# A decoder layer on one core: the order of work ahead of the attention loop

## The chip, the cores and the metric

The kernel runs on one core of a Trainium2 chip. The metric is device time in microseconds (us), the median of several executions; lower is better. TensorE does matrix products, VectorE, ScalarE and GpSimd (called POOL in the profile) the rest, SyncE issues most transfers. Each engine runs its own list of instructions in order and waits on semaphores for the others.

## The reference

Sixteen sequences of 128 tokens with 128 features go through three sub-layers, each followed by a layer norm:

- a linear attention with a feed-forward part (`_L0_attn_ref`): `x1 = layernorm(x + attn(x))`;
- a cross attention on `ctx_1024` with 16 heads of 8 features. Queries and keys are normalised per head, the queries rotated by position and scaled, then softmax and values;
- a mixture of 8 experts, of which each token takes two.

```python
q = _layernorm(q, qn_w, qn_b)
k = _layernorm(k, kn_w, kn_b)
q = _apply_rope(q) * scale
attn = jnp.einsum('bhqd,bhkd->bhqk', q, k)
attn = jax.nn.softmax(attn, axis=-1)
o = jnp.einsum('bhqk,bhkd->bhqd', attn, v)
```

## The kernel before

Everything is float32 outside the score products. The 16 sequences are four groups (`G = 4`) of four; a group's tile is 128 partitions x 512 columns. Cross attention's queries pass these steps per group `g`, all on tensors of 128 x 512:

- VectorE `first_sum(g)` adds the first sub-layer's output and takes the means and variances of x1; ScalarE `inv_std(2, g)` makes 1/std by Ln and Exp (L854, L856); VectorE `normalise_x1(g)` writes N in four operations (L1089);
- TensorE `x1_T(g)` transposes N (L410), ScalarE `copy_x1T(g)` copies it to LNT (L896), TensorE `queries(g)` projects (L565);
- ScalarE `square(1, g, ...)` writes V (the projection with its bias, L869) and its square into QP (L870); TensorE `variances(1, g)` averages the square per head (L482); ScalarE `head_inv_std(1, g)` makes 1/std by Ln and Exp on KP (L874, L876); VectorE `head_norm(1, g)` multiplies V by KP (L1109);
- POOL `query_affine(g)` applies the norm's weight and bias to V (L1433) and forms V times cos in ADD (L1435); TensorE `rotate(g)` multiplies V by the rotation matrix (L575); VectorE `add_rotation(g)` multiplies that by sin (`times_sin`, L1175) and adds it to ADD (L1183);
- the result is split into three bfloat16 parts: ScalarE `high_part` (L884) and `middle_part` (L888), POOL `low` (L1411, L1413). SyncE writes the parts to a scratch in HBM (L347) and reads them back packed as QPK (L354, `read_packed`). The keys took the same way before, into KPK.

The attention is done in 64 units, four per sequence `b`: unit `u` is a quarter of the heads of sequence `u // 4`. For each unit the scores are computed twice. First as `scores_for_max` (L650), four products per unit, two units at a time; VectorE `maxima(u)` reduces them to the row maxima M (L1204). After a sequence's four units TensorE `max_T(b)` transposes M (L667), ScalarE `negate_max(b)` writes NEGM (L977) and issues its transfer into a row of QPK (L980), which then carries the negated maximum. After that come `scores(u, m)` (L685), whose products include this row, and ScalarE takes Exp (L1019); `times_v` (L707) multiplies with the values. The maxima run `LEAD = 12` units ahead: 12 units are done ahead of the loop, and in the loop each `scores(u, u + LEAD)` computes unit `u`'s scores and unit `u + 12`'s scores for the maximum.

A rule on banks sets the turns ahead of the loop: the scores for the maxima have two PSUM banks, so `scores_for_max(u)` waits until `maxima(u - 1)` is done (s_max), the first pair also until the packed keys and queries of group 0 have landed. `max_T(b)` waits for maxima `4b + 3` and for the negation of `b - 1`.

`keep_clock(n)` issues n products of the identity with itself into a bank of its own (L416); they compute nothing that is used. The order on each engine is written out by hand: TensorE's at L748 to L772, ScalarE's behind its last table load at L983, VectorE's in the loop over LEAD at L1279.

```python
if u >= 2:
    pe.wait_ge(s_max, u - 1)
```

(from `wait_for_max(u)`, called for `u` and `u + 1` ahead of each pair.)

Of the kernel before, what the change touches and what calls it, by code (L numbers as in the profile page):

```python
# [94 lines left out]
def decoder_layer(nc, x, ctx_in, attn_w, w1, w2, col_params, row_params, xw, eW1, eb1, eW2, eb2, consts, ones_row,  # L95
# [6 lines left out]
    with ExitStack() as ctx:  # L102
# [3 lines left out]
        def sem(name):  # L106
            return ctx.enter_context(nc.semaphore(name))
# [59 lines left out]
        QBC, KBC, B2C = (cols[:, i:i + 1] for i in range(16, 19))  # L167
# [42 lines left out]
        def cs(g):  # L210
            return slice(g * W, (g + 1) * W)

        def blk(t, b):
            return t[:, b * P:(b + 1) * P]
# [7 lines left out]
        def head_bank(t, g):  # L222

            return ((1, 1, 2, 3)[g] if t else (6 if g < G - 1 else 0))

        def var_bank(t, g):

            return (0, 0, 4, 5)[g] if t else (7 if g < G - 1 else 1)

        def x1_bank(g):  # L230

            return (0, 0, 4, 5)[g]

        def rot_bank(g):

            return (1, 6, 4, 6)[g]
# [55 lines left out]
        s_qc = sem("s_qc"); s_rot = sem("s_rot"); s_t1 = sem("s_t1"); s_t2 = sem("s_t2"); s_qh = sem("s_qh")  # L292
# [111 lines left out]
        def _(pe):  # L404
            mm = nc.tensor.matmul

            def transposes(bank, src, g, done, k=GB):

                for j in range(k):
                    last = nc.tensor.transpose(ps[:, bank, j * P:(j + 1) * P], blk(src, g * GB + j), K["ident"])  # L410
                last.then_inc(done, 1)

            def keep_clock(n, bank=7):

                for _ in range(n):
                    mm(ps[:, bank, 0:P], K["ident"], K["ident"], start=True, stop=True)  # L416
# [61 lines left out]
            def variances(t, g):  # L478
                pe.wait_ge(s_sq[t], g + 1)
                if t == 0:  # L480
                    pe.wait_ge(s_vaug, g + 1)
                mm(ps[:, var_bank(t, g), :], K["mean8"], SQ[t][:, cs(g)], start=True, stop=True).then_inc(s_var[t], 1)  # L482
# [72 lines left out]
            def x1_T(g):  # L555
                pe.wait_ge(s_norm[2], g + 1)
                if g >= 2:
                    pe.wait_ge(s_g1, NF * G)
                transposes(x1_bank(g), N, g, s_nT[2])

            def queries(g):
                pe.wait_ge(s_lnT[2], g + 1)
                if g >= 2:
                    pe.wait_ge(s_g2, g + 1)
                mm(ps[:, head_bank(1, g), :], XWT[:, 0, :], LNT[:, cs(g)], start=True, stop=True).then_inc(s_qc, 1)  # L565

            def rotate(g):
                pe.wait_ge(s_aff[1], g + 1)
                if g == 1:
                    pe.wait_ge(s_g1, NF * G)  # L570
                if g == 2:
                    pe.wait_ge(s_lv[1], 3)
                if g == 3:
                    pe.wait_ge(s_t2, 2)
                mm(ps[:, rot_bank(g), :], K["rotate"], V[:, cs(g)], start=True, stop=True).then_inc(s_rot, 1)  # L575
# [58 lines left out]
            def wait_for_max(u):  # L634

                b = u // 4
                if u % (4 * GB) == 0:
                    pe.wait_ge(s_pack[0][b // GB], 32)
                    pe.wait_ge(s_pack[1][b // GB], 32)
                if u == 0:  # L640
                    pe.wait_ge(s_lv[1], 2)
                if u == 1:
                    pe.wait_ge(s_sq[1], 2)
                if u >= 2:
                    pe.wait_ge(s_max, u - 1)

            def score_for_max(u, j):
                b, par, half = max_unit(u)
                t = slice(b * P, (b + 1) * P)
                last = mm(ps[:, u % 2, j * P:(j + 1) * P], QPK[HALF * par:HALF * par + KROWS, 4 * half + j, t],  # L650
                          KPK[HALF * par:HALF * par + KROWS, 4 * half + j, t], start=True, stop=True)
                if j == 3:
                    last.then_inc(s_sm, 1)

            def scores_for_max(u):

                wait_for_max(u)
                wait_for_max(u + 1)
                for j in range(4):
                    score_for_max(u, j)  # L660
                    score_for_max(u + 1, j)

            def max_T(b):
                pe.wait_ge(s_max, 4 * (b + 1))
                if b >= 1:
                    pe.wait_ge(s_negm, b)
                nc.tensor.transpose(ps[0:H, 7, 0:P], M[:, b % RING, :], K["ident"]).then_inc(s_mT, 1)  # L667
# [79 lines left out]

            pe.wait_ge(s_g1, NF * G)  # L748
            x1_T(2)
            keep_clock(6)  # L750
            queries(2)
            scores_for_max(0)
            keep_clock(4)
            scores_for_max(2)
            keep_clock(3)
            x1_T(3)
            variances(1, 2)
            scores_for_max(4)
            keep_clock(2)
            queries(3)  # L760
            scores_for_max(6)
            keep_clock(3)
            max_T(0)
            variances(1, 3)
            scores_for_max(8)
            pe.wait_ge(s_negm, 1)
            keep_clock(3)
            max_T(1)
            scores_for_max(10)
            pe.wait_ge(s_negm, 2)  # L770
            keep_clock(4)
            rotate(2)  # L772
            for u in range(4 * B):
                b, r = divmod(u, 4)
                scores(u, u + LEAD)
# [71 lines left out]
        def _(act):  # L847
            A = nc.scalar.activation

            def inv_std(n, g, eps):  # L850

                act.wait_ge(s_mv[n], g + 1)
                b = slice(g * GB, (g + 1) * GB)
                A(lnv[:, n, b], mv[:, n, b, 1], ACT.Ln, bias=eps).then_inc(s_lnv[n], 1)  # L854
                act.wait_ge(s_lnv[n], g + 1)
                A(rstd[:, n, b], lnv[:, n, b], ACT.Exp, scale=-0.5).then_inc(s_rstd[n], 1)  # L856
# [9 lines left out]
            def square(t, g, done_mm, bias):  # L866
                act.wait_ge(done_mm, g + 1)
                if t == 1:
                    A(V[:, cs(g)], ps[:, head_bank(t, g), :], ACT.Identity, bias=bias)  # L869
                A(SQ[t][:, cs(g)], ps[:, head_bank(t, g), :], ACT.Square, bias=bias).then_inc(s_sq[t], 1)  # L870

            def head_inv_std(t, g):
                act.wait_ge(s_var[t], g + 1)
                A(RS[t][:, cs(g)], ps[:, var_bank(t, g), :], ACT.Ln, bias=1e-6).then_inc(s_lv[t], 1)  # L874
                act.wait_ge(s_lv[t], g + 1)
                A(RS[t][:, cs(g)], RS[t][:, cs(g)], ACT.Exp, scale=-0.5).then_inc(s_rs[t], 1)  # L876

            def high_part(t, g):
                act.wait_ge((s_aff[0], s_qh)[t], g + 1)
                if g >= 2:  # L880
                    act.wait_ge(s_scr[t][g % 2], 16 * len(TERMS_K) * (g // 2))
                if t == 1 and g < 2:
                    act.wait_ge(s_scr[0][g % 2], 16 * len(TERMS_K) * (G // 2))
                nc.scalar.copy(PART[:, g % 2, 0, :], (KN, ADD)[t][:, cs(g)]).then_inc(s_hi[t], 1)  # L884

            def middle_part(t, g):
                act.wait_ge(s_r1[t], g + 1)
                nc.scalar.copy(PART[:, g % 2, 1, :], (KQ, KP)[t][:, cs(g)]).then_inc(s_mid[t], 1)  # L888
# [5 lines left out]
            def copy_x1T(g):  # L894
                act.wait_ge(s_nT[2], g + 1)
                nc.scalar.copy(LNT[:, cs(g)], ps[:, x1_bank(g), :]).then_inc(s_lnT[2], 1)  # L896
# [85 lines left out]

            copy_x1T(2)  # L983
            high_part(1, 1)
            inv_std(2, 3, 1e-5)
            square(1, 2, s_qc, QBC)
            middle_part(1, 1)
            copy_x1T(3)
            head_inv_std(1, 2)
            square(1, 3, s_qc, QBC)  # L990
            negate_max(0)
            head_inv_std(1, 3)
# [77 lines left out]
        def _(dve):  # L1070
# [14 lines left out]
            def normalise(dst, src, n, g, ready, done):  # L1085
                dve.wait_ge(ready, g + 1)
                for j in range(GB):
                    b = g * GB + j
                    last = ts(dst(b), src(b), mv[:, n, b, 0:1], rstd[:, n, b:b + 1], ALU.subtract, ALU.mult)  # L1089
                last.then_inc(done, 1)  # L1090
# [79 lines left out]
            def normalise_x1(g):  # L1170
                normalise(lambda b: blk(N, b), lambda b: blk(LNT, b), 2, g, s_rstd[2], s_norm[2])
# [94 lines left out]
            def place(g):  # L1266
# [9 lines left out]
                step(nc.vector.tensor_reduce(HH, rank[:, :, :], AX.X, ALU.add))  # L1276
                nc.vector.tensor_copy(posu[:, bs], HH).then_inc(s_pos, 1)

            for u in range(LEAD):  # L1279
                maxima(u)  # L1280
                if u == 1:
                    normalise_x1(3)
                if u == 5:
                    head_norm(1, 2, QBC)
                if u == 8:
                    head_norm(1, 3, QBC)
            add_rotation(2)
            for u in range(4 * B):
# [313 lines left out]
```

## Time and profile before

| | us |
|---|---|
| median of 3 runs | 318.08 (318.07 to 318.13) |
| the profiled execution | 315.94 |
| its span, first to last instruction | 313.9 |
| TensorE busy | 259.9 |
| VectorE busy | 182.2 |
| ScalarE busy | 152.5 |
| POOL busy | 109.2 |

The median is what counts; the profiled execution is one run with the profiler on, and its span is what the views show. Busy times of the engines overlap. The chain that ended last is the work followed back from the last instruction, at each step to what released it; 63% of the span is TensorE's on it, 10% VectorE's, 9% ScalarE's and 6% transfers. In a timeline "x4" means that four like instructions were merged; a float32 product shows as two records, so an identity product counts 2. Two operations of an engine can overlap by about 0.1 us in the records. "issue" in the chain is time in which the engine waited for nothing that the profile shows; a wait for a transfer may be put down to it.

### The profile page before, as it was taken

How to read it: one execution, taken by the hardware profiler on the slowest of the kernel's cores; microseconds unless marked ns; L12 is line 12 of the kernel's file. 1: busy time of each engine (PE TensorE's matmuls, PEld its weight loads, DVE VectorE, ACT ScalarE, POOL GpSimd, SP SyncE). 2: the span in 40 equal slices, each digit the busy share in tenths (PEclk: the TensorE clock that was granted, in tenths of full speed). 3: DMA queues.
4: the chain of work that ended last, by engine and by line, in shares of the span. 5: the costliest groups of instructions: out<-in, count | busy, mean ns of one | idle time of the engine just before them, and what ended most of it. 6: DMA issues, size and time to landing. Idle time of an engine off the chain costs nothing.

```text
span 313.9 us, 7318 instructions
## 1 busy us (share of the span) xinstructions
PE 259.9 (83%) x2359; PEld 191.9 (61%) x2359; DVE 182.2 (58%) x649; ACT 152.5 (49%) x375; POOL 109.2 (35%) x164
## 2 busy tenths in 40 slices
PE   0697877968999997799988998981699999999980
PEld 0376755843453445445554555681699999999970
DVE  4732474872034466687769788568056666666660
ACT  2234216446689784367666767520044444444430
POOL 4000003720432441546400815755124444434431
PEclk9999999999999999989999999996599999999997
DMA  7910203530599775436790001151222200000000
GB/s 209 294 43 0 72 0 101 151 51 1 148 216 179 281 148 136 70 82 122 219 194 4 3 3 39 37 154 34 60 60 70 68 17 17 17 20 14 3 16 17
DMA packets 26641, 26.43 MB, mean 84 GB/s; under 512 B 2895, under 2 KB 23120, under 8 KB 26610
## 3 DMA queue, kind: packets, MB, share of 16 engines
q1 hardware_dynamic: 24996, 23.25, 31.2%
q0 software_dynamic: 1328, 2.75, 2.5%
q8 instruction: 16, 0.26, 0.4%
q14 instruction: 13, 0.11, 0.1%
q10 hardware_dynamic: 288, 0.07, 0.1%
HBM read 16.93 MB, written 9.29 MB: 84 GB/s over the span
## 4 chain that ended last, share of the span: by engine, by line
PE 63%; DVE 10%; ACT 9%; DMA 6%; issue 5%; POOL 2%; SPq 1%; ACTq 1%; POOLq 1%; DVEq 0%
PE ps L842 11%; PE ps L831 10%; PE ps L685 4%; PE ps L416 4%; PE ps L707 4%; PE ps L584 3%; DMA WA<-in_attn_w_dram 3%; DMA QPK<-NEGM 2%; PE ps L438 2%; PE ps L551 2%; PE ps L410 2%; PE ps L482 2%; DVE N L1089 2%; PE ps L575 2%; PE ps L723 2%
## 5 line engine op out<-in xcount | busy, mean ns | idle before, releaser
L1204 DVE TENSOR_REDUCE M<-ps 128x4 f32<-128x512 f32 x64 | 42.8, 685 | 14.9 <-PE ps L650 14.2
L1019 ACT ACTIVATE CTX<-ps 128x512 f32<-128x512 f32 x64 | 37.6, 602 | 23.7 <-PE ps L685 16.9
L1060 ACT ACTIVATE KPK<-ps,EB 128x128 f32<-128x128 f32 x80 | 24.6, 358 | 37.6 <-PE ps L831 33.8
L831 PE MATMUL ps<-QPK,EW 128*128 x320 | 39.6, 277 | 0.4 <-ACT QPK L1045 0.4
L842 PE MATMUL ps<-EW,KPK 128*128 128x128 f32 x320 | 39.4, 276 | 0.0
L831 PEld LDWEIGHTS ps<-QPK,EW 128*128 128x128 f32 x320 | 37.8, 194 | 0.8 <-issue 0.8
L1536 POOL DMA_INDIRECT out_dram<-ADD,tok_u x21 | 21.0, 1002 | 49.3 <-DVE ADD L1370 49.3
L842 PEld LDWEIGHTS ps<-EW,KPK 128*128 128x128 f32 x320 | 37.2, 191 | 0.0
L416 PE MATMUL ps<-C 128*128 128x128 f32 x178 | 27.8, 301 | 7.1 <-DMA sorted_scratch<-KVS,posu 7.1
L416 PEld LDWEIGHTS ps<-C 128*128 128x128 f32 x178 | 23.7, 205 | 10.5 <-issue 9.9
L685 PE MATMUL ps<-QPK,KPK 49*128 49x128 bf16 x256 | 25.4, 221 | 2.7 <-ACT CTX L1019 1.6
L650 PE MATMUL ps<-KPK,QPK 48*128 48x128 bf16 x256 | 23.1, 221 | 4.2 <-DVE M L1204 2.2
L685 PEld LDWEIGHTS ps<-QPK,KPK 49*128 49x128 bf16 x256 | 14.6, 95 | 14.7 <-issue 10.1
L1378 DVE TENSOR_SCALAR KPK<-ps,EB 128x128 f32<-128x128 f32 x80 | 22.3, 336 | 0.5 <-PE ps L831 0.5
L1516 POOL DMA_INDIRECT sorted_scratch<-KVS,posu x16 | 15.6, 976 | 19.3 <-PE ps L685 8.5
L650 PEld LDWEIGHTS ps<-KPK,QPK 48*128 48x128 bf16 x256 | 13.3, 95 | 7.7 <-DVE M L1204 4.9
L410 PE MATMUL ps<-C,N 128*128 128x128 f32 x48 | 8.5, 305 | 11.1 <-DVE N L1089 11.0
L1384 DVE SCALAR_TENSOR_TENSOR ADD<-ps,ADD 128x128 f32<-128x128 f32 x20 | 5.8, 291 | 17.5 <-PE ps L842 16.6
L551 PE MATMUL ps<-LNT,W 128*128 128x512 f32 x32 | 14.6, 595 | 0.9 <-ACT QPK L952 0.9
L410 PEld LDWEIGHTS ps<-C,N 128*128 128x128 f32 x48 | 6.0, 153 | 13.3 <-issue 8.6
L707 PE MATMUL ps<-CTX,VA 128*32 128x128 f32 x256 | 13.9, 285 | 0.0
L1166 DVE TENSOR_TENSOR LNT<-ps,X 128x512 f32<-128x512 f32 x4 | 2.8, 689 | 18.8 <-PE ps L410 18.8
(215 smaller groups left out, 492.6 us busy)
## 6 DMA issues: line engine op xcount, KB each, us to landing
k_packed_scratch<-PART SPq DMA_DIRECT2D x24, 128.0 KB, 2.4
KPK<-k_packed_scratch SPq DMA_DIRECT2D x8, 384.0 KB, 6.5
q_packed_scratch<-PART SPq DMA_DIRECT2D x24, 128.0 KB, 2.8
QPK<-q_packed_scratch SPq DMA_DIRECT2D x8, 384.0 KB, 5.7
EW<-in_eW_dram SPq DMA_DIRECT2D x1, 2048.0 KB, 12.4
KPK<-sorted_scratch SPq DMA_DIRECT2D x24, 66.0 KB, 1.9
X<-in_x_dram SPq DMA_DIRECT2D x4, 256.0 KB, 4.2
C<-in_constants_dram SPq DMA_DIRECT2D x1, 720.0 KB, 6.2
```

Source lines behind the costliest of these rows:

```text
L416: mm(ps[:, bank, 0:P], K["ident"], K["ident"], start=True, stop=True)
L551: mm(ps[:, 4 + c, :], W1[:, c * P:(c + 1) * P], LNT[:, cs(g)], start=True, stop=True).then_inc(s_f1, 1)
L650: last = mm(ps[:, u % 2, j * P:(j + 1) * P], QPK[HALF * par:HALF * par + KROWS, 4 * half + j, t], KPK[HALF * par:HALF * par + KROWS, 4 * h ...
L685: last = mm(ps[:, 2 + u % 2, j * P:(j + 1) * P], KPK[HALF * par:HALF * par + KROWS + 1, 4 * half + j, t], QPK[HALF * par:HALF * par + KROW ...
L707: last = mm(ps[TILE * j:TILE * (j + 1), 5 + b % 2, half * P:(half + 1) * P], VA[b // 8][:, c:c + TILE], EXPS[:, u % 4, j * P:(j + 1) * P], ...
L831: last = mm(ps[:, c // 2, (c % 2) * P:(c % 2 + 1) * P], EW1[:, e, (c % NF) * P:(c % NF + 1) * P], XST[:, bass.ds(t * P, P)], start=True, s ...
L842: last = mm(ps[:, 4, 0:P], HE[:, c, :], EW2[:, e, c % NF, :], start=(c == 0), stop=(c == 2 * NF - 1))
L1019: A(EXPS[:, u % 4, :], ps[:, 2 + u % 2, :], ACT.Exp).then_inc(s_exp, 1)
L1060: last = A(HE[:, c, :], ps[:, k, (c % 2) * P:(c % 2 + 1) * P], ACT.Relu, bias=EB1[:, h, c:c + 1])
L1204: nc.vector.tensor_reduce(M[:, b % RING, c:c + 4], bank_rows(u % 2), AX.X, ALU.max).then_inc(s_max, 1)
L1378: last = ts(HE[:, NF + c, :], ps[:, 2 + k, (c % 2) * P:(c % 2 + 1) * P], EB1[:, (h + 1) % NE, c:c + 1], 0.0, ALU.add, ALU.max)
L1536: pool.indirect_dma_start(out_rows, bass.IndirectOffsetOnAxis(ap=tok_u[:, 0:1], axis=0), OUTN[:, :], None, bounds_check=last_row, oob_is_e ...
```

## The change

Three lists of instructions are reordered and `keep_clock` is redistributed; nothing else changes.

```diff
--- before.py
+++ after.py
@@ -747,29 +747,29 @@
 
             pe.wait_ge(s_g1, NF * G)
             x1_T(2)
-            keep_clock(6)
+            keep_clock(3)
             queries(2)
+            keep_clock(5)
+            variances(1, 2)
+            keep_clock(2)
+            x1_T(3)
             scores_for_max(0)
-            keep_clock(4)
+            queries(3)
             scores_for_max(2)
-            keep_clock(3)
-            x1_T(3)
-            variances(1, 2)
+            keep_clock(2)
             scores_for_max(4)
-            keep_clock(2)
-            queries(3)
-            scores_for_max(6)
-            keep_clock(3)
             max_T(0)
             variances(1, 3)
-            scores_for_max(8)
+            scores_for_max(6)
             pe.wait_ge(s_negm, 1)
             keep_clock(3)
+            rotate(2)
+            scores_for_max(8)
             max_T(1)
+            pe.wait_ge(s_negm, 2)
+            keep_clock(3)
             scores_for_max(10)
-            pe.wait_ge(s_negm, 2)
-            keep_clock(4)
-            rotate(2)
+            keep_clock(2)
             for u in range(4 * B):
                 b, r = divmod(u, 4)
                 scores(u, u + LEAD)
@@ -982,11 +982,11 @@
 
             copy_x1T(2)
             high_part(1, 1)
+            square(1, 2, s_qc, QBC)
             inv_std(2, 3, 1e-5)
-            square(1, 2, s_qc, QBC)
             middle_part(1, 1)
+            head_inv_std(1, 2)
             copy_x1T(3)
-            head_inv_std(1, 2)
             square(1, 3, s_qc, QBC)
             negate_max(0)
             head_inv_std(1, 3)
@@ -1276,13 +1276,12 @@
                 step(nc.vector.tensor_reduce(HH, rank[:, :, :], AX.X, ALU.add))
                 nc.vector.tensor_copy(posu[:, bs], HH).then_inc(s_pos, 1)
 
+            normalise_x1(3)
             for u in range(LEAD):
                 maxima(u)
                 if u == 1:
-                    normalise_x1(3)
-                if u == 5:
                     head_norm(1, 2, QBC)
-                if u == 8:
+                if u == 7:
                     head_norm(1, 3, QBC)
             add_rotation(2)
             for u in range(4 * B):
```

On TensorE, behind `x1_T(2)` (its transposes are the first row): L416 is `keep_clock`, L565 `queries`, L482 `variances(1, 2)`, the second L410 `x1_T(3)`, and L650 x8 a pair of scores for the maxima. The last two rows are `queries(2)` and the first pair before, `queries(3)` and the second pair now.

```order
 L410 MATMUL ps<-C,N 128x128 x4
-L416 MATMUL ps<-C 128x128 x6
+L416 MATMUL ps<-C 128x128 x3
+L565 MATMUL ps<-LNT,XWT 128x512
+L416 MATMUL ps<-C 128x128 x5
+L482 MATMUL ps<-QP,C 128x512
+L416 MATMUL ps<-C 128x128 x2
+L410 MATMUL ps<-C,N 128x128 x4
+L650 MATMUL ps<-KPK,QPK 128x128 x8
 L565 MATMUL ps<-LNT,XWT 128x512
 L650 MATMUL ps<-KPK,QPK 128x128 x8
```

The first scores moved from behind `queries(2)` to behind `variances(1, 2)` and `x1_T(3)`; `queries(3)` moved up from between the third and the fourth pair to between the first and the second.

On TensorE just ahead of the loop, whose first `scores` is L685: L667 is `max_T(1)` and L575 `rotate(2)`. The L650 x8 in both is the sixth pair before and the fifth now; the one with a + is the sixth now.

```order
 L416 MATMUL ps<-C 128x128 x3
-L667 MATMUL ps<-C,M 16x128
+L575 MATMUL ps<-V,C 128x512
 L650 MATMUL ps<-KPK,QPK 128x128 x8
-L416 MATMUL ps<-C 128x128 x4
-L575 MATMUL ps<-V,C 128x512
+L667 MATMUL ps<-C,M 16x128
+L416 MATMUL ps<-C 128x128 x3
+L650 MATMUL ps<-KPK,QPK 128x128 x8
+L416 MATMUL ps<-C 128x128 x2
 L685 MATMUL ps<-QPK,KPK 128x128
```

`rotate(2)` moved from between the last pair and the loop to ahead of the fifth pair, and the identity products at the entry are three ahead of the sixth pair and two behind it, where four stood behind it.

On VectorE, behind the statistics of group 3 (L1082): L1204 is `maxima`, L1089 `normalise_x1(3)`, L1109 `head_norm`.

```order
 L1082 BN_AGGR mv<-st 128x2 x4
-L1204 TENSOR_REDUCE M<-ps 128x4 x2
 L1089 TENSOR_SCALAR N<-LNT,mv,rstd 128x128 x4
-L1204 TENSOR_REDUCE M<-ps 128x4 x4
+L1204 TENSOR_REDUCE M<-ps 128x4 x2
 L1109 TENSOR_TENSOR V<-V,KP 128x512
-L1204 TENSOR_REDUCE M<-ps 128x4 x3
+L1204 TENSOR_REDUCE M<-ps 128x4 x6
 L1109 TENSOR_TENSOR V<-V,KP 128x512
```

The normalisation stands ahead of all maxima; `head_norm(1, 2)` is behind the second maximum instead of the sixth, and `head_norm(1, 3)` behind the eighth instead of the ninth.

## Rows read from the trace of the kernel before

**Rows 1.** The page, part 2: TensorE's granted clock in 40 equal slices.
```profile
PEclk9999999999999999989999999996599999999997
```

**Rows 2.** The chain that ended last: start us, length us, what (xcount).
```profile
117.19 1.97 issue
...
122.28 0.44 PE ps L410 x4
...
128.91 0.64 ACT KP L876
129.57 0.69 DVE V L1109
```

**Rows 3.** Windows: stretch, us, busy PE, PEld, DVE, ACT, POOL, PEclk, DMA, GB/s.
```profile
129.00:131.00 2.00, 0.19 (x2) 0.02 (x1) 1.29 (x2) 0.69 (x2) 0.64 (x1) 1.00 0.04 6
...
132.20:135.60 3.40, 3.40 (x22) 1.70 (x21) 1.62 (x3) 0.60 (x1) 0.28 (x1) 0.50 0.00 0
```

**Rows 4.** Timeline to the second scores: start us, us, engine line op.
```profile
114.82 1.50 PE L416 MATMUL ps<-C 128*128 128x128 f32 x12
...
115.02 0.58 ACT L896 COPY LNT<-ps 128x512 f32<-128x512 f32 x1 [0.17 <-PE ps L410]
...
116.16 1.02 PE L565 MATMUL ps<-LNT,XWT 128*128 128x512 f32 x2
...
117.69 0.20 ACT L856 ACTIVATE rstd<-lnv 128x4 f32<-128x4 f32 x1
117.81 0.67 ACT L869 ACTIVATE V<-ps,cols 128x512 f32<-128x512 f32 x1
118.37 0.68 ACT L870 ACTIVATE QP<-ps,cols 128x512 f32<-128x512 f32 x1
...
119.16 0.40 PE L650 MATMUL ps<-KPK,QPK 48*128 48x128 bf16 x8 [1.97 <-issue]
...
119.58 1.29 DVE L1204 TENSOR_REDUCE M<-ps 128x4 f32<-128x512 f32 x2 [2.16 <-PE ps L650]
...
120.79 1.11 DVE L1089 TENSOR_SCALAR N<-LNT,mv,rstd 128x128 f32<-128x128 f32 x4
...
121.01 0.40 PE L650 MATMUL ps<-KPK,QPK 48*128 48x128 bf16 x8 [0.36 <-DVE M L1204]
```

**Rows 5.** Timeline: VectorE's normalisation and POOL's operations near it.
```profile
111.86 1.40 DVE L1089 TENSOR_SCALAR N<-LNT,mv,rstd 128x128 f32<-128x128 f32 x4
112.05 0.89 POOL L1433 TENSOR_SCALAR V<-V,cols 128x512 f32<-128x512 f32 x1 [2.17 <-DVE V L1109]
...
119.64 1.16 POOL L1413 TENSOR_TENSOR PART<-KP,PART 128x512 bf16<-128x512 f32 x1 [2.12 <-ACT PART L888]
```

**Rows 6.** Timeline at the loop's entry.
```profile
127.08 1.15 ACTq L980 DMA_DIRECT2D QPK<-NEGM  x1
...
131.01 0.40 PE L650 MATMUL ps<-KPK,QPK 48*128 48x128 bf16 x8 [1.82 <-DVE M L1204]
...
131.34 1.31 PE L416 MATMUL ps<-C 128*128 128x128 f32 x8
...
132.44 1.92 PE L575 MATMUL ps<-V,C 128*128 128x512 f32 x2
...
134.29 0.28 PE L685 MATMUL ps<-QPK,KPK 49*128 49x128 bf16 x1
...
134.39 0.69 DVE L1175 TENSOR_TENSOR QP<-ps,C 128x512 f32<-128x512 f32 x1 [1.68 <-PE ps L575]
...
135.80 1.28 DVE L1204 TENSOR_REDUCE M<-ps 128x4 f32<-128x512 f32 x2
```

**Rows 7.** SyncE's timeline of group 1's and 3's reads; chain at 157 us.
```profile
123.14 1.23 SPq L354 DMA_DIRECT2D QPK<-q_packed_scratch  x2
...
154.12 1.22 SPq L354 DMA_DIRECT2D QPK<-q_packed_scratch  x2
...
157.23 7.70 DMA QPK<-NEGM
```

## The prediction

> **What bounds the kernel now.** I read four views, in this order. First the page: its slices of the granted clock show TensorE at 9 in all but four of 40; the first of the four, an 8, is the eighteenth slice, 133 to 141 us, where the kernel enters its attention loop [rows 1]. Then the chain of waits around that place. It lies on TensorE, with three kinds of piece between: 1.97 us of waiting until the packed queries of group 0 had landed, then group 3's head variances (ScalarE's Ln and Exp on KP, 0.6 us each), then VectorE's product V times KP that stands between two maxima [rows 2]. The last of these counts: `head_norm(1, 3)` starts at 129.57, as soon as ScalarE has its 1/std, and the ninth `maxima` waits behind it. TensorE, whose next scores need ten maxima, is idle 1.82 us and starts at 131.01 [rows 6].
>
> Third the windows: from 129 to 131 us TensorE was busy for 0.19 us; from 132.2 to 135.6 its granted clock was 0.50, so 1.2 GHz instead of 2.4 [rows 3]. The price shows in one operation: `rotate(2)` takes 1.92 us at 132.44, where the product of the same size in `queries(2)` took 1.02 at 116.16 [rows 4, 6]. Last the timeline, for lengths and order. The first scores start at 119.16, the second pair at 121.01: one turn (scores, two maxima, a semaphore) is 1.85 us [rows 4]. Six pairs need five turns and the first maximum of the last, 5 x 1.85 + 0.42 + 0.61 + 0.14 = 10.4 us; the loop could start at 129.6. It starts at 134.29 [rows 6]. So 4.7 us are lost to waits, slow clock and work laid in the wrong place.
>
> **The change, walked through.** I move each instruction to where its inputs let it start, with lengths of the same operation.
>
> Start. `x1_T(2)` is as before, so the identity products begin at 114.82. Six took 1.34 us up to 116.16, 0.22 each [rows 4]; three are done at 115.5. `queries(2)` then waits only for ScalarE's copy, over at 115.60, and runs 115.65 to 116.67 instead of from 116.16: 0.5 earlier. ScalarE now squares group 2 first: V at 116.7, the square 0.56 behind it and 0.68 long [rows 4], done at 117.95. `inv_std(2, 3)` (two of 0.20) comes after it, at 118.3 instead of 117.89: the price of that swap is 0.4. VectorE was idle then, so `normalise_x1(3)` costs its own length, 1.11 alone [rows 4] or 1.40 beside POOL [rows 5]; POOL's second part of group 1 now falls on it, so I take the middle: done at 119.55. TensorE fills with five products and `variances(1, 2)`, over before 119.2, then two more. `x1_T(3)` starts at 119.7 and takes 0.44 [rows 2], and the first scores start at 120.15. Before it was 119.16: **1.0 us lost**. The packed queries, which set 119.16, have landed by then.
>
> Turns. `queries(3)` needs the copy of group 3, which ScalarE makes after Ln and Exp for group 2 (119.2 to 120.4): copy to 121.0, queries 121.1 to 122.05. The second scores could start at 120.15 + 1.85 = 122.0, so this costs 0.05. `head_norm(1, 2)` (0.69) lies in the gap in which VectorE waits for those scores: nothing. Third scores at 123.9, fourth at 125.75, with `max_T(0)` and `variances(1, 3)` between them while VectorE takes maxima. ScalarE issues the row of block 0 at 124.85; that instruction took 1.15 [rows 6] and Ln and Exp for group 3 stand behind it: done at 127.25. `head_norm(1, 3)` starts after the eighth maximum, 127.45, and ends at 128.15. Three products and `rotate(2)` run 126.1 to 127.8 under the maxima; fifth scores at 127.8 instead of 127.6, 0.2 lost. Sixth at 129.65. `scores(0)` needs eleven maxima: 129.65 + 0.42 + 0.61 + 0.14 is 130.85. The walk is 120.15 + 5 x 1.85 + 0.25 + 1.2. Against 134.29 that is **3.45 us earlier**, made of the idle 1.82 gone, `rotate(2)` (1.92) and four products (1.1 from 131.34) off the entry, 1.0 and 0.4 of the turns lost again.
>
> Into the loop. Before, `rotate(2)` ended just ahead of the loop, and from VectorE's `times_sin(2)` at 134.39 to its next maximum at 135.80 are 1.41 us, 1.51 behind the loop's start [rows 6]. Now `times_sin(2)` waits for the twelfth maximum, 131.35, and the thirteenth starts at 132.75, 1.9 behind the start. So **0.4 is given back**, while `rotate(3)` at full clock hides in it; ScalarE's second Exp, behind the cast of VectorE's sum (`high_part(1, 2)`), moves with VectorE. From the thirteenth maximum on both kernels run the same instructions, 3.05 us apart. SyncE's transfers of groups 2 and 3 hang on that cast and shift with it. There are 25 identity products before and 20 now; the last two lie in the 0.9 us in which TensorE waits for the eleventh maximum.
>
> Sum: +1.0 late first scores, -4.45 of waits and entry work, +0.4 into the loop: -3.05. Profiled execution: 315.94 (span 313.9) to 312.9. The runs' median, 318.08, is 2.1 above the profiled one; I subtract from the median: **315.0 us**. Ends: if group 3's statistics and the normalisation go faster than walked, and the loop gives nothing back, -4.2; if each of the eight links from `queries(2)` to the first scores costs 0.1 more, -2.2.
>
> **Rivals.**
>
> A. *The clock falls all the same.* TensorE now waits about 0.6, then 1.0 us between pairs; 1.82 idle came before the fall, but 1.97 at 117.19 came before none [rows 2, 6], so a length of idling alone does not tell. For: little work is added there. Against: no wait is above 1.0, and the fillers sit in the gaps. A stretch like the one seen (3.4 us at 0.50, all busy [rows 3]) loses half, 1.7: -1.35, 316.7 us. Chance 0.11.
>
> B. *The row of block 0 lands late.* `scores(0)` needs NEGM's row in QPK. It is issued at 124.85 instead of 127.08, now inside the reads of group 1's queries, which SyncE issued at 123.14 [rows 7]. The trace has a row that landed 7.70 us after its issue, at 157.23, three us behind such a pair of reads [rows 7]. At that price it lands at 132.55, 1.7 after 130.85: 316.7 us. Against: group 1's parts are ready earlier, and in the trace of before a row issued 4 us behind the same reads had landed by 134.29. Chance 0.08. The Trainium skill (DMA: Bandwidth & Descriptors, Issuing engines are not separate DMA queues) says that transfers from all issuing engines run on the same 16 DMA engines and interleave, which speaks for this rival; the 7.70 agrees.
>
> C. *VectorE's normalisation stands behind POOL.* If POOL's 1.16 us operation [rows 5] took turns with it whole, `normalise_x1(3)` would end near 120.9, and all after it come 1.4 later: 316.4 us. Against: at 111.86 the four took 1.40 instead of 1.11 with POOL's 0.89 us beside them, a loss of 0.3 and not of 0.9 [rows 4, 5]. Chance 0.04. The Trainium skill (SBUF — State Buffer, SBUF: two separate sides) has VectorE and GpSimd share a port pair as an exclusive lock for a whole instruction; by that rule the loss should have been the larger one, and the trace shows the smaller.
>
> D. *Slower: the clock falls in the waits after the first scores and stays low until the loop.* Between 120.15 and 130.85 TensorE has six groups of scores (0.33 from 131.01 to the next row [rows 6]), three products of 0.9, two `max_T` and ten identity products: 7.3 us of work in 10.7. At half clock it is 7.3 more, of which up to 3.4 goes into idle time: 3.9 to 7.3, take 5. Against a gain of 3.05 that is +1.95: 320.0 us. It decides once more than 3.05 us of slow work lies on the chain. For: five fewer fillers and a wait that follows every pair. Against: the only low stretch here ended after 3.4 us of busy TensorE. Chance 0.07.
>
> E. *No change: the loop gives the time back.* It waits for the row issued at 157.23, which is on the chain. If that landing is set by the traffic and the traffic does not move, the gain stops there: 318.1. Against: those transfers start with a cast that moves. Chance 0.06.
>
> **How the numbers follow.** My forecast has 0.64. Faster by over 0.2% (0.64 us, about what a measurement tells from no change) are forecast, A, B and C: 0.87. Within: E, 0.06. Slower: D, 0.07. The range takes the forecast's own ends nearly whole (a tenth of it outside) and A, B and C: 313.9 to 317.1; outside are D, E and those tails, 0.2.
>
> **What would show it.** First scores near 120.1 and `normalise_x1(3)` ahead of the first maximum; then pairs 1.85 to 2.05 apart, without a gap of 1.8; `rotate(2)` near 1.0 us between fourth and fifth scores; clock 1.00 from 114 to 140; `scores(0)` near 130.9; the row that took 7.70 issued near 154.2. I am wrong if the clock is 0.50 anywhere there, if the first scores come after 121, or if the loop starts by 131.5 and the end moves by less than 2.

## The result, and the profile after

| | before | after |
|---|---|---|
| median of 4 runs, us | 318.07 (316.07 to 318.13) | 313.02 (312.82 to 313.42) |
| profiled execution, us | 315.94 | 313.18 |
| its span, us | 313.9 | 311.1 |

The ratio is 0.9858, 95% interval 0.9818 to 0.9898: faster. The medians moved by 5.05 us, below the low end of my range (313.9); the two profiled executions moved by 2.8, and 3.05 was forecast for them. Every ratio below leaves out the executions that took over 1.5% longer than the quickest one of the same kernel on the same chip.

The page of the kernel after: the low slice where the loop is entered is gone [rows 1].

```profile
span 311.1 us, 7298 instructions
...
PE 257.3 (83%) x2349; PEld 189.8 (61%) x2349; DVE 183.1 (59%) x649; ACT 152.8 (49%) x375; POOL 109.5 (35%) x164
...
PEclk9999999999999999999999999997599999999996
```

The timeline after (start us, length us, engine, line, operation) answers to [rows 4 to 6].

```profile
118.27 2.04 DVE L1089 TENSOR_SCALAR N<-LNT,mv,rstd 128x128 f32<-128x128 f32 x4 [1.03 <-ACT rstd L856]
...
118.81 1.16 POOL L1412 TENSOR_TENSOR PART<-KP,PART 128x512 bf16<-128x512 f32 x1 [1.48 <-ACT PART L888]
...
120.95 0.40 PE L650 MATMUL ps<-KPK,QPK 48*128 48x128 bf16 x8
...
122.82 0.40 PE L650 MATMUL ps<-KPK,QPK 48*128 48x128 bf16 x8
...
124.67 0.40 PE L650 MATMUL ps<-KPK,QPK 48*128 48x128 bf16 x8 [0.81 <-DVE M L1204]
...
127.63 1.02 PE L575 MATMUL ps<-V,C 128*128 128x512 f32 x2
...
131.71 0.21 PE L685 MATMUL ps<-QPK,KPK 49*128 49x128 bf16 x1 [0.21 <-DVE M L1204]
...
133.47 0.68 DVE L1204 TENSOR_REDUCE M<-ps 128x4 f32<-128x512 f32 x1
```

The normalisation is ahead of the maxima, but took 2.04 us with POOL's operation beside it. The first scores start at 120.95, then the pairs are 1.85 to 1.87 apart, 2.05 from the fourth to the fifth, `rotate(2)` takes 1.02 between the fourth and the fifth, and `scores(0)` starts at 131.71. In the chain the wait for packed queries, group 3's 1/std and `head_norm(1, 3)` [rows 2] have given way to the normalisation and the turns:

```profile
118.27 2.06 DVE N L1089 x4
...
120.36 0.66 PE ps L410 x4
...
130.88 1.28 DVE M L1204 x2
132.16 0.61 DVE QP L1175
```

To compare kernels I measure from the first identity product behind `x1_T(2)` to the thirteenth maximum; the rest of this text calls that **the entry**. Before, from 114.82 to 135.80, it took 20.98 us at a mean granted clock of 0.92; after, 18.84 at 1.00. A stretch at half clock, about 0.50, I call a low stretch. First the two windows before, then the two after (stretch, us, busy PE, PEld, DVE, ACT, POOL, PEclk, DMA, GB/s):

```profile
114.82:135.80 20.98, 16.81 (x133) 10.61 (x132) 13.69 (x32) 8.62 (x18) 6.38 (x6) 0.92 0.54 100
...
200.00:230.00 30.00, 19.46 (x166) 16.94 (x167) 16.16 (x79) 6.86 (x19) 13.37 (x16) 0.77 0.27 76
```

```profile
114.63:133.47 18.84, 15.44 (x124) 9.35 (x123) 14.61 (x32) 8.74 (x18) 6.39 (x6) 1.00 0.61 110
...
200.00:230.00 30.00, 19.34 (x154) 17.71 (x152) 16.90 (x79) 6.28 (x20) 13.21 (x17) 0.83 0.26 76
```

So of the 2.8 us 2.14 are in the entry. 0.19 lay ahead of it already, and about 0.5 came behind the tail's wait, where the clock is low in both kernels and came back sooner after (0.83 against 0.77 from 200 to 230 us); neither is work that the change touched. From the thirteenth maximum to the last Exp of the loop both took 66.4 us. The row that took 7.70 us [rows 7] moved with the loop, as forecast:

```profile
154.63 8.02 DMA QPK<-NEGM
```

Open were two things: what the entry lost against the walk's 3.05, and where the median found 2.2 us that the profiled executions do not show. All this is read from one profiled execution of each kernel.

### The profile page after: what moved, and what is told of

It reads as the page before. It is cut to its first block, busy times and chain, and to the rows that moved or that the text cites. A ratio compares the mean times of both kernels' runs of the same rounds, so it can differ in the third digit from the quotient of the medians.

```text
span 311.1 us, 7298 instructions
## 1 busy us (share of the span) xinstructions
PE 257.3 (83%) x2349; PEld 189.8 (61%) x2349; DVE 183.1 (59%) x649; ACT 152.8 (49%) x375; POOL 109.5 (35%) x164
## 4 chain that ended last, share of the span: by engine, by line
PE 61%; DVE 14%; ACT 9%; DMA 5%; issue 4%; POOL 2%; ACTq 1%; POOLq 1%; DVEq 0%; SPq 0%
PE ps L842 11%; PE ps L831 10%; PE ps L685 4%; PE ps L707 4%; PE ps L416 4%; PE ps L584 3%; DVE N L1089 3%; DMA QPK<-NEGM 3%; PE ps L438 2%; PE ps L551 2%; PE ps L410 2%; DVE M L1204 2%; PE ps L482 2%; DVE st L1077 2%; PE ps L723 2%
## 5 line engine op out<-in xcount | busy, mean ns | idle before, releaser
L1204 DVE TENSOR_REDUCE M<-ps 128x4 f32<-128x512 f32 x64 | 42.7, 685 | 13.3 <-PE ps L650 12.3
L416 PE MATMUL ps<-C 128*128 128x128 f32 x168 | 26.4, 300 | 7.6 <-DMA sorted_scratch<-KVS,posu 7.2
L416 PEld LDWEIGHTS ps<-C 128*128 128x128 f32 x168 | 22.7, 206 | 11.8 <-issue 10.9
L685 PE MATMUL ps<-QPK,KPK 49*128 49x128 bf16 x256 | 25.1, 218 | 3.9 <-ACT CTX L1019 1.6
L650 PE MATMUL ps<-KPK,QPK 48*128 48x128 bf16 x256 | 22.9, 218 | 1.2 <-DVE M L1204 1.2
L685 PEld LDWEIGHTS ps<-QPK,KPK 49*128 49x128 bf16 x256 | 14.3, 94 | 14.7 <-issue 9.8
L410 PE MATMUL ps<-C,N 128*128 128x128 f32 x48 | 8.5, 306 | 12.1 <-DVE N L1089 12.0
L650 PEld LDWEIGHTS ps<-KPK,QPK 48*128 48x128 bf16 x256 | 13.0, 94 | 4.0 <-DVE M L1204 3.7
L410 PEld LDWEIGHTS ps<-C,N 128*128 128x128 f32 x48 | 5.9, 153 | 14.5 <-issue 8.8
L707 PE MATMUL ps<-CTX,EW 128*32 128x128 f32 x256 | 13.6, 285 | 0.0
```

The costliest lines, as they stand in the source:

```text
L685: last = mm(ps[:, 2 + u % 2, j * P:(j + 1) * P], KPK[HALF * par:HALF * par + KROWS + 1, 4 * half + j, t], QPK[HALF * par:HALF * par + KROW ...
L707: last = mm(ps[TILE * j:TILE * (j + 1), 5 + b % 2, half * P:(half + 1) * P], VA[b // 8][:, c:c + TILE], EXPS[:, u % 4, j * P:(j + 1) * P], ...
L1204: nc.vector.tensor_reduce(M[:, b % RING, c:c + 4], bank_rows(u % 2), AX.X, ALU.max).then_inc(s_max, 1)
```

## The experiments

Sixteen runs follow, four per chip, on four chips, which I call A to D. A ratio is against the kernel before on the same chip. The entry of a run is that of its one profiled execution.

### Chip A: fill the waits, move one thing

`b_warm`, the kernel before with both long waits filled:

```diff
 queries(2)
+keep_clock(8)
...
 max_T(1)
+keep_clock(8, 6)
 scores_for_max(10)
```

> The kernel before, in its own order, with 16 identity products added in TensorE's two longest waits: 8 behind queries(2), where it waits for the packed queries, and 8 (into bank 6) behind max_T(1), where it was idle 1.82 us. Nothing else moves. Theory K (the clock: the executions of the kernel before at 318.1 have one low stretch more than the profiled one at 315.9, and the changed kernel has none ahead of the loop): no low stretch from 114 to 140 us, the loop starts 1.0 to 1.8 us earlier than 134.29, and the median falls from 318.1 to about 314.3, with no second value near 318. Rival T (the 2.1 us lie in transfers or in the tail, and only the low stretch seen in the profile is saved): median 316.3 to 316.8. Rival O (only the order of work counts; fillers do nothing): 318.1.

Ratio 0.9873 (0.9832 to 0.9914), with the order of the work untouched. All six executions had a mean clock of 0.969 or 0.970; of the 28 of the kernel before on this chip, 24 lay between 0.933 and 0.964 and four lower. The entry took 20.38 at full clock. The median fell by as much as theory K said (318.2 against 322.3, both longer than in the first comparison; see under chips C and D). K's other number was missed: counted from the first identity product, `scores(0)` came 0.6 us earlier than in the first profile of before, not 1.0 to 1.8. Chip A has no profile of the kernel before, so where its executions lost the 4 us is not shown.

`b_rotate`:

```diff
 max_T(1)
+rotate(2)
 scores_for_max(10)
...
 keep_clock(4)
-rotate(2)
```

> The kernel before with one edit: rotate(2) stands behind max_T(1), in the 1.82 us wait, instead of behind the last identity products at the entry. Theory K and my walk: 0.9 us (its length at full clock) comes off the entry, and if the clock then stays up another 1.0 to 1.8: loop start at 131.6 to 133.4, median 315.2 to 316.2. Rival (the group 3 part of the change carries nearly all): median at most 0.5 below 318.1.

Ratio 0.9878 (0.9844 to 0.9912), more than the 2 to 3 us expected. The entry took 19.70: 0.5 less than the 20.15 to 20.17 that the old order takes at full clock (below), and half of the wait is filled. On chip D the same edit gained less, as the table there shows.

`a_nofill`:

```diff
 pe.wait_ge(s_negm, 2)
-keep_clock(3)
 scores_for_max(10)
-keep_clock(2)
```

> The changed kernel without the five identity products at the loop's entry (three ahead of the sixth pair of scores, two behind it); the wait for the second negation stays. Theory: the waits there are 0.2 to 0.7 us and the clock was 1.00 throughout, so without fillers either nothing changes (313.0 within 0.3) or the clock falls at the entry and it costs 1 to 2 us (314 to 315). If these five carry the gain, the second.

Ratio 0.9972 (0.9935 to 1.0009): no gain that can be told from none, and 0.85% or 2.7 us above `a_middle_late` on the same chip, where the changed kernel itself did not run. Its profiled execution shows the fall. First the timeline, then the window behind it:

```profile
130.56 0.40 PE L650 MATMUL ps<-KPK,QPK 48*128 48x128 bf16 x8 [1.26 <-DVE M L1202]
131.82 0.21 PE L685 MATMUL ps<-QPK,KPK 49*128 49x128 bf16 x1 [0.85 <-DVE M L1202]
...
132.96 2.07 PE L575 MATMUL ps<-V,C 128*128 128x512 f32 x2
```

```profile
132.40:179.50 47.10, 47.08 (x483) 25.16 (x483) 24.57 (x43) 22.14 (x46) 11.49 (x11) 0.50 0.46 103
```

Behind waits of 1.26 and 0.85 us the clock fell, `rotate(3)` took 2.07, and it stayed low for 47 us of busy loop. That execution took 333.97 us, one of three of the thirteen near 334; ten took 318.7 to 325.0. So the 47 us are what a fall there can turn into, not what it mostly costs. The entry itself took 18.83, as in the changed kernel: the five products add no time to it and protect what follows. My text had their place right ("in the 0.9 us in which TensorE waits") and no price for them.

`a_middle_late`:

```diff
-middle_part(1, 1)
 head_inv_std(1, 2)
+middle_part(1, 1)
 copy_x1T(3)
```

> The changed kernel with ScalarE's middle_part(1, 1) behind head_inv_std(1, 2), so that POOL's second part of group 1 starts about 1.2 us later and no longer beside VectorE's normalise_x1(3), which took 2.04 us there instead of 1.11. Theory L (the two share a port and take turns): the normalisation takes 1.1 to 1.4, the first scores start about 0.7 us earlier than 120.95, and the median falls by 0.5 to 0.8 to about 312.4. Rival (the normalisation is slow for another cause, or the turns absorb it): 2.0 again, or 1.1 with the median unchanged at 313.0.

Ratio 0.9887 (0.985 to 0.9925). The timeline:

```profile
118.52 1.11 DVE L1089 TENSOR_SCALAR N<-LNT,mv,rstd 128x128 f32<-128x128 f32 x4 [1.03 <-ACT rstd L856]
...
120.28 0.40 PE L650 MATMUL ps<-KPK,QPK 48*128 48x128 bf16 x8
...
121.67 1.12 PE L565 MATMUL ps<-LNT,XWT 128*128 128x512 f32 x2 [1.00 <-ACT LNT L896]
...
131.86 0.23 PE L685 MATMUL ps<-QPK,KPK 49*128 49x128 bf16 x1 [0.45 <-DMA QPK<-NEGM]
```

With POOL out of the way the normalisation takes 1.11 and the first scores come 0.9 earlier in the entry. Most of it is lost: `queries(3)` waits behind the moved cast, and `scores(0)` waits 0.45 us for the row of block 0, rival B's mechanism. The entry took 18.50, so 0.34 us of the 0.93 is kept.

### Chip B: the same kernels again, and POOL alone

`b_again` is the kernel before, `a_again` the changed one.

> The kernel before, unchanged, for a second profiled execution and its spread of times. Theory K (the clock falls in different places from one execution to the next): the profile shows low stretches ahead of or in the loop that differ from 132.2 to 135.6, and the mean granted clock of its executions spreads by 0.01 or more, the slower ones at the lower clock. Rival F (a fixed difference between the profiled execution and the others): the same stretch as in the first profile, all other executions at one time.

> The changed kernel, unchanged, on the same chip. Theory K: its executions lie closer together than those of the kernel before, at a mean clock near 0.97, and the ratio of the medians is 0.984 to 0.988. My walk alone (3.05 us less in each execution) would give 0.990 to 0.991.

Against the runs of before, `b_again` gave 0.9966 (0.9925 to 1.0006), no difference, and `a_again` 0.9909 (0.9872 to 0.9946). The second profile of the kernel before, timeline and windows:

```profile
120.44 0.40 PE L650 MATMUL ps<-KPK,QPK 48*128 48x128 bf16 x8 [2.42 <-issue]
120.76 2.08 PE L416 MATMUL ps<-C 128*128 128x128 f32 x8
122.77 0.61 PE L650 MATMUL ps<-KPK,QPK 48*128 48x128 bf16 x8
...
133.38 0.40 PE L650 MATMUL ps<-KPK,QPK 48*128 48x128 bf16 x8 [1.81 <-DVE M L1204]
...
134.95 1.91 PE L575 MATMUL ps<-V,C 128*128 128x512 f32 x2
```

```profile
118.00:120.40 2.40, 0.01 (x1) 0.00 (x0) 0.25 (x4) 2.07 (x5) 0.35 (x1) 1.00 1.05 203
120.90:124.30 3.40, 3.40 (x21) 2.98 (x22) 3.15 (x8) 0.00 (x0) 0.72 (x1) 0.51 0.43 116
...
134.30:137.70 3.40, 3.40 (x24) 1.76 (x22) 1.48 (x4) 0.26 (x1) 0.56 (x1) 0.52 0.00 0
```

It has **two** low stretches ahead of the loop: one at 134.3, as in [rows 3], and one behind the wait for the packed queries, 2.42 us here, in which four identity products (2.08 us) hold back the second scores. Its entry took 22.66, against 20.98 with one. The executions agree: the quickest of the kernel before here took 314.15 at a mean clock of 0.976, most some 316 to 318.5 at 0.960 to 0.971. Theory K holds in that the clock falls in different places from one execution to the next; rival F falls. That K expected `a_again` at 0.984 to 0.988 was wrong: the changed kernel had slower executions too (313.06 to 316.16 us at 0.960 to 0.975), and here gained what the walk had given. The two profiled executions on this chip, 318.21 and 313.70, differ by 4.5 us, and 3.8 of them lie in the entry.

`a_rotate_back`:

```diff
 keep_clock(3)
-rotate(2)
 scores_for_max(8)
...
 keep_clock(2)
+rotate(2)
```

> The changed kernel with rotate(2) put back to just ahead of the loop, behind the last two identity products. What is left of the change is group 3's part and the identity products. Theory (my walk): rotate(2) at full clock costs the entry 0.9 us less the 0.2 that TensorE waits there for the eleventh maximum, and saves 0.2 at the fifth scores; times_sin(2) comes at about 132.6 instead of 132.07: 0.4 to 0.7 slower than the changed kernel, no more. Rival (rotate(2) ahead of the fifth pair is what holds the clock): a low stretch at the entry, 1.5 to 3 slower.

Ratio 0.9899 (0.9862 to 0.9936), the entry 18.94 against 18.83, no low stretch. `rotate(2)` at the entry costs 0.1 us once the clock is up, because VectorE's twelfth maximum ends no sooner. That is less than the 0.4 to 0.7 expected, far less than the 1.92 in my sum, and in the run times nothing: the ratio is no higher than that of `a_again`.

`a_pool_wait`:

```diff
 pool.wait_ge(s_mid[t], g + 1)
+if t == 1 and g == 1:
+    pool.wait_ge(s_norm[2], G)
```

> The changed kernel with POOL's second operation of low(1, 1) made to wait until normalise_x1(3) is done; ScalarE's order stays. Theory L (VectorE's four operations take 2.04 us because POOL's runs beside them): they take 1.1 now, the first scores start 0.8 us earlier, queries(3) 0.6 to 0.8 earlier, the loop starts near 131.0 instead of 131.7, unless the row of block 0, which the late-middle kernel waited 0.45 us for, holds it: median 0.3 to 0.8 below the changed kernel's. Rival (the row's landing sets the entry now): loop start within 0.2 of 131.7 and the median within 0.2.

Ratio 0.9855 (0.98 to 0.991), below `a_again` by about 0.5%, with overlapping intervals. The timeline:

```profile
119.75 1.11 DVE L1089 TENSOR_SCALAR N<-LNT,mv,rstd 128x128 f32<-128x128 f32 x4 [1.03 <-ACT rstd L856]
...
121.51 0.40 PE L650 MATMUL ps<-KPK,QPK 48*128 48x128 bf16 x8
```

1.11 again, and the entry took 17.99, 0.84 less than `a_again`. My walk had it at 132.75 - 114.82 = 17.93. Theory L holds, by the length of the normalisation and of the entry; the row of block 0 was in time.

### Chips C and D: one wait filled at a time

`b_fill_first` and `b_first_2` have only `keep_clock(8)` behind `queries(2)`; `b_fill_second` and `b_second_2` only `keep_clock(8, 6)` behind `max_T(1)`; `a_third` is the changed kernel, `b_rotate_2` the same as `b_rotate`.

> The kernel before with 8 identity products added behind queries(2), in the wait for the packed queries, and nothing else. Theory K (in some executions of the kernel before the clock falls behind this wait, as in the second profile, and in most behind the wait of 1.82 us at 131): the first low stretch is gone, the second stays in the profile. The median falls by 0.5 to 2 us, by how often the first occurred on this chip. Rival (fillers do nothing unless the wait next to the loop is filled): no change.

> The kernel before with 8 identity products into bank 6 behind max_T(1), in the wait of 1.82 us ahead of the sixth pair, and nothing else. Theory K: no low stretch at the loop's entry, rotate(2) takes 1.0 us, the loop starts 1.3 to 1.8 us earlier against the first scores; the median falls by 1.5 to 2; what is left of the spread comes from the first wait. Rival: as for the other.

> The kernel before with 8 identity products behind queries(2), again, now on one chip with the three kernels below. Theory W1 (what the median gained beyond the walk's 3 us is a fall of the clock behind the wait of 2 to 2.5 us for the packed queries, which the changed kernel does not have): most of the extra, 1 to 3 us below before, and more than the kernel with the second wait filled. Rival W2 (it is the wait of 1.82 us ahead of the sixth pair): 0 to 0.5 us.

> The kernel before with 8 identity products in the wait of 1.82 us, again. Theory W1: 0 to 1.5 us below before, and its slower executions have a low stretch behind the first wait. Rival W2: 2 us or more, and more than the kernel above.

> The changed kernel once more, beside the kernels with one wait filled. The walk's 3 us plus what W1 and W2 give on this chip: 3 to 5.5 us below before. If it gains no more than the better of the two filled kernels, the order of the work was worth nothing and the clock everything.

> The kernel before with rotate(2) in the second wait, again. It fills half of that wait and takes 0.9 to 1.9 us off the entry. On another chip it gained as much as the changed kernel had on the first (0.988). W1: if this chip lets the clock fall behind the first wait, 1 to 2 us below before and no more; W2: 3 us or more, as on the other chip.

| kernel | chip | ratio (interval) | median of all, us (before) | entry, us | low stretch in it |
|---|---|---|---|---|---|
| b_fill_first | C | 0.9880 (0.9847 to 0.9913) | 319.74 (323.27) | 21.28 | behind the second wait |
| b_fill_second | C | 0.9969 (0.9926 to 1.0011) | 322.49 (323.27) | 23.14 | behind the first wait |
| b_first_2 | D | 0.9972 (0.9941 to 1.0002) | 319.95 (321.38) | 20.17 | none |
| b_second_2 | D | 0.9883 (0.9826 to 0.9941) | 320.28 (321.38) | 20.15 | none |
| b_rotate_2 | D | 0.9944 (0.9901 to 0.9987) | 321.34 (321.38) | 19.66 | none |
| a_third | D | 0.9918 (0.9884 to 0.9953) | 318.89 (321.38) | 18.84 | none |

By the ratios the first filled wait brought the gain on C and the second on D. C is clear. D, where W1 and W2 were put to the test, is not: the six executions of `b_second_2` ran from 316.22 to 329.88 us and its ratio rests on three of them, while over all executions `b_first_2` is no slower. The ratio of `b_rotate_2`, too, rests on six of twelve; over all twelve it gained nothing. So W1 against W2 stays open. Where a wait stayed open, the profile could show the fall behind it, and filled waits never did. `b_fill_first`, then `b_fill_second`:

```profile
119.71 0.40 PE L650 MATMUL ps<-KPK,QPK 48*128 48x128 bf16 x8 [0.61 <-issue]
...
131.56 0.40 PE L650 MATMUL ps<-KPK,QPK 48*128 48x128 bf16 x8 [1.81 <-DVE M L1205]
...
132.88 1.91 PE L575 MATMUL ps<-V,C 128*128 128x512 f32 x2
```

```profile
121.22 0.61 PE L650 MATMUL ps<-KPK,QPK 48*128 48x128 bf16 x8 [2.53 <-issue]
121.76 2.07 PE L416 MATMUL ps<-C 128*128 128x128 f32 x8
...
137.00 1.02 PE L575 MATMUL ps<-V,C 128*128 128x512 f32 x2
```

`rotate(2)` took 1.91 behind the open second wait and 1.02 behind the filled one; four identity products took 2.07 behind the open first wait, and there the clock stayed at half for twice as long as in `b_again`, 6.8 us.

The expectation for `a_third` (3 to 5.5 us) was a little high: 0.8% is 2.6. It had also said that a gain no greater than that of the better filled kernel would leave nothing to the order of the work. By the ratios this is so (0.9918 against 0.9883, intervals overlapping); over all executions `a_third` is 1.1 and 1.4 us below the two. What the order is worth in run time is therefore not shown; in the profiled entries it is.

All twelve profiles of chips A, C and D show something near the end of the loop that the six others do not: another low stretch, ahead of the tail's long wait. In eight of them it stands behind an idle time of ScalarE of 3.0 to 3.2 us, for whose Exp TensorE waits; in the other four it begins between 193 and 198 us with TensorE busy. In `a_third`, ScalarE's and TensorE's timelines and the window:

```profile
202.56 1.08 ACT L1019 ACTIVATE CTX<-ps 128x512 f32<-128x512 f32 x2 [3.04 <-remote]
...
203.22 0.60 PE L685 MATMUL ps<-QPK,KPK 49*128 49x128 bf16 x4 [2.39 <-ACT CTX L1019]
...
202.00:208.80 6.80, 5.58 (x43) 4.26 (x44) 2.86 (x13) 2.51 (x7) 3.15 (x4) 0.50 0.18 61
```

From the thirteenth maximum to the loop's last Exp these twelve took 68.8 us or more, the six others 65.5 to 66.4. It strikes both orders, so it is no part of the change, but it makes up much of the longer times on these chips and lowers the mean clock. What holds ScalarE up the profile does not show.

The last two, on C, combine findings. `a_fill` is the changed kernel with twelve more products in its five waits:

```diff
-keep_clock(2)
+keep_clock(5)
 x1_T(3)
 scores_for_max(0)
+keep_clock(2)
...
-keep_clock(2)
+keep_clock(5)
 scores_for_max(4)
...
 variances(1, 3)
+keep_clock(2, 6)
...
 max_T(1)
+keep_clock(2, 6)
```

> The changed kernel with 12 identity products more, in its five remaining waits of 0.3 to 0.8 us ahead of the loop; no other change. Theory K (the slower executions of the changed kernel, at a mean clock of 0.960 to 0.971, have low stretches too): the executions move together at 0.973 to 0.976, the best one stays as it was, and the median falls by 0.5 to 1.5. Rival (they come from the loop or the tail, or the added products delay the work behind them): the median stays within 0.3 or rises.

`a_best` has the same, but three products ahead of `x1_T(3)` instead of five, and POOL's wait of `a_pool_wait`.

> The changed kernel with POOL's second operation of low(1, 1) held until normalise_x1(3) is done, and 10 identity products more in the waits. Theory: both effects add: the loop starts 0.7 us earlier against the kernel's queries(2) than in the changed kernel, no low stretch ahead of the tail, and the median is 0.5 to 1 below the other kernel with fillers, 1.5 to 2 below the changed kernel. Rival (POOL's hold costs elsewhere, the packed rows of group 1 and the negated maxima landing later): no better than the other kernel with fillers.

`a_fill`: ratio 0.9824 (0.979 to 0.9857), the entry 18.83 as in the changed kernel, so the added products delay nothing. The changed kernel itself did not run on this chip, so what they gain is not separated. The mean clocks, 0.943 to 0.970, missed the 0.973 to 0.976 expected; the low stretch near 200 us is in this profile too. `a_best`: 0.9787 (0.975 to 0.9824), the lowest ratio of all kernels here, 0.4% below `a_fill` with overlapping intervals (four of its six executions took 315.9 to 316.8 us, two over 331), and the entry 18.00. Its timeline:

```profile
120.07 0.40 PE L650 MATMUL ps<-KPK,QPK 48*128 48x128 bf16 x8
...
130.82 0.21 PE L685 MATMUL ps<-QPK,KPK 49*128 49x128 bf16 x1 [0.21 <-DVE M L1207]
```

## Why the prediction was right and wrong

**The entry, step by step.** `queries(2)`, the square and `inv_std(2, 3)` came within 0.2 us of the walk (1/std done at 118.24, walked 118.3). The six pairs took 10.76 us from the first scores to `scores(0)`, walked 10.70, and the thirteenth maximum followed 1.76 behind, walked 1.9. One link failed: "POOL's second part of group 1 now falls on it, so I take the middle: done at 119.55". It was done at 120.31. I had priced the overlap from one neighbour, the 1.40 beside POOL's one-input operation [rows 5], and taken less than even that; beside the two-input one it was 2.04, one of the four taking 1.27 instead of 0.34. That is rival C, to which I gave 0.04 with 1.4 us; it occurred, at 0.84 by `a_pool_wait`. The rule of the Trainium skill (SBUF — State Buffer, SBUF: two separate sides), an exclusive lock for a whole instruction, agrees with this and with `a_pool_wait`, and not with the 1.40 beside the one-input operation; my sentence that the trace spoke against it rested on that one pair. The single operation in VectorE's timeline after:

```profile
118.78 1.27 DVE L1089 TENSOR_SCALAR N<-LNT,mv,rstd 128x128 f32<-128x128 f32 x1
```

**The split of the gain** was wrong. I took `rotate(2)` (1.92) and four products (1.1) off the entry as work. `a_rotate_back` shows 0.1 for the first at full clock. Profiles of the old order at full clock (`b_first_2`, `b_second_2`: the kernel before with one wait filled) have an entry of 20.15 to 20.17 against the changed kernel's 18.84: **in the entry the order is worth 1.3 us**, and 2.2 with POOL held. The rest is the clock: one low stretch costs 0.8 (20.98), two cost 2.5 (22.66).

**The median: the step that failed.** "The runs' median, 318.08, is 2.1 above the profiled one; I subtract from the median." This took the difference for a constant and the gain for the same in every execution. It is neither. The changed kernel's entry took 18.83 or 18.84 in all three profiles of it, with no low stretch. The kernel before, in its two profiles, took 20.98 and 22.66, a gain of 2.1 or 3.8 by how often the clock falls. The 1.97 at 117.19 stood in my text as a wait behind which nothing fell, and I priced the removal of that wait as "1.0 us lost" at the first scores. It is one of the two falls: filling it alone gained 1.2% on C (and 0.3%, not clear of none, on D). That the first comparison's three executions of the kernel before at 318.1 had both stretches fits the 2.1 us but is argued, not shown: none of the three was profiled, and their clocks are not on record. `b_again`, with both stretches, took 318.21; yet only 1.7 us of the difference to 315.94 lie in its entry, and 0.8 ahead of it at full clock. The delay near 200 us, about 3 us, would cost as much or more. Against it speaks that on each chip either every profile shows it or none, and the first comparison's two do not; no run settles it. What the runs show is that the same change gives 0.9858, 0.9909 and 0.9918 in three comparisons, and the forecast's own ratio (315.0 / 318.08 = 0.990) lies inside the last two intervals, and just outside the first.

**The rivals.** A did not occur in the changed kernel's profiles ahead of the loop, but without the entry's fillers it did (`a_nofill`). B occurred only where ScalarE's part of group 1 was delayed (`a_middle_late`, 0.45 us). C occurred. D and E did not: the far row moved with the loop.

## What to carry to other kernels

Before pricing a reordering around long waits of TensorE, ask for the spread of the kernel's executions and their mean clock: a difference between profiled execution and median can be a stretch that falls in most executions and not in the one you hold, and a change that closes the wait gains it. Fill each wait of a latency-bound stretch with products that are ready anyway and check that they end before the wait does. An operation placed into another engine's idle time is free only if no third engine holds what it needs: look for what runs beside it, by its number of inputs.

## What was not expected of the hardware

- The same wait of TensorE let its clock fall to half in some executions and not in others: 1.82 us at 129 to 131 before the fall to 0.50 in the first profile, none behind the same 1.82 in `b_first_2`; 2.42 and 2.53 us in front of a fall in `b_again` and `b_fill_second`, 2.14 to 2.47 without one in `b_second_2`, `b_rotate` and `b_rotate_2`.
- In `a_nofill` the granted clock stayed at 0.50 for 47 us with TensorE busy throughout, mostly in the loop's small score and value products; in `b_rotate` it did so for 20 us, from 167 to 187.
- VectorE's four normalising operations took 1.11 alone, 1.40 beside a POOL operation with one tensor input, 2.04 to 2.05 beside one with two, the same in every profile.
